# Attention output kept by feature and divided by its softmax sums in the dense stages, with two PSUM banks for the sums of y

## The reference

```python
x = x + attn_a(layernorm(x), W_attn, W_proj)    # softmax(causal q k^T / 4), times a decay by distance, times v, times W_proj
x = x + ffn(layernorm(x), w1, b1, w2, b2)       # weights binarised: sign(w) * mean|w| of the row; exact gelu
x = x + attn_b(layernorm(x), Wq, bq, ..., Wo, bo, gamma, beta)   # softmax(causal), times v, times Wo, layernorm of the result
x = x + ffn(layernorm(x), w1, b1, w2, b2)
```

## Time and profile before

| | |
|---|---|
| median of 3 runs | 2737.45 us (2736.65 to 2740.8) |
| the profiled execution | 2736.11 us, span 2734.4 us |
| granted TensorE clock, mean | 0.959 |
| PE busy | 2454.8 us, 90% |
| DVE busy | 1958.3 us, 72% |
| ACT busy | 1515.6 us, 55% |
| POOL busy | 1052.5 us, 38% |
| DMA | 171.03 MB, mean 63 GB/s |

### The profile page before, as it was taken

How to read it: one execution, slowest core, us unless ns; L and a number is a source line. 1 busy time by engine, 2 the same in 40 slices (tenths; PEclk the granted TensorE clock), 3 DMA queues, 4 the chain that set the end, 5 groups by cost and what they waited for, 6 DMA issues and landing times. The chain is left out here.

```text
span 2734.4 us, 44488 instructions
## 1 busy us (share of the span) xinstructions
PE 2454.8 (90%) x13984; PEld 1404.0 (51%) x13984; DVE 1958.3 (72%) x4863; ACT 1515.6 (55%) x3309; POOL 1052.5 (38%) x1274
## 2 busy tenths in 40 slices
PE   4959999999999999969997599999999999997788
PEld 2535545454544545437774355555555555553676
DVE  5667787777787777716663588888888888870786
ACT  1218576776767685734332056666666666664333
POOL 0037777777777777751221301000101001011653
PEclk8969999999999999989998589999999999998999
DMA  4994142332505050033544751423505234102110
GB/s 134 252 144 63 24 56 36 44 51 32 70 11 75 13 69 6 5 114 77 125 96 98 111 75 16 64 38 44 70 15 72 32 51 62 18 7 99 47 54 31
DMA packets 181847, 171.03 MB, mean 63 GB/s; under 512 B 90352, under 2 KB 131056, under 8 KB 180848
## 3 DMA queue, kind: packets, MB, share of 16 engines
q1 hardware_dynamic: 181616, 168.18, 35.0%
HBM read 105.98 MB, written 61.08 MB: 61 GB/s over the span
## 5 line engine op out<-in xcount | busy, mean ns | idle before, releaser
L704 POOL TENSOR_TENSOR att_a_wd<-att_a_wt,decay 128x256 f32<-128x256 f32 (+3 forms) x896 | 754.6, 873 | 259.8 <-PE att_a_po L907 122.7
L742 ACT ACTIVATE att_b_wt<-att_b_ps 128x512 f32<-128x512 f32 (+3 forms) x1280 | 589.4, 539 | 354.6 <-PE att_b_ps L882 352.6
L782 DVE TENSOR_REDUCE att_a_mpart<-att_a_pm 128x1 f32<-128x512 f32 x768 | 513.5, 687 | 132.2 <-PE att_a_pm L860 129.0
L782 DVE TENSOR_REDUCE att_b_mpart<-att_b_pm 128x1 f32<-128x512 f32 x768 | 503.7, 686 | 109.7 <-PE att_b_pm L860 107.7
L860 PE MATMUL att_a_pm<-att_a_kop,att_a_qop 128*128 128x512 f32 (+3 forms) x1280 | 522.6, 426 | 55.6 <-DMA att_a_qop<-att_a_qop 28.2
L742 ACT ACTIVATE att_a_wt<-att_a_ps 128x512 f32<-128x512 f32 (+3 forms) x896 | 430.8, 506 | 218.1 <-PE att_a_ps L885 131.6
L860 PE MATMUL att_b_pm<-att_b_kop,att_b_qop 128*128 128x512 f32 (+3 forms) x1280 | 503.0, 408 | 36.6 <-DMA att_b_qop<-att_b_qop 29.9
L882 PE MATMUL att_b_ps<-att_b_qop,att_b_kop 128*128 128x512 f32 (+3 forms) x1280 | 453.2, 383 | 6.6 <-ACT att_b_wt L742 3.4
L722 POOL TENSOR_SCALAR_AFFINE_SELECT att_b_wt<-att_b_wt 128x512 f32<-128x512 f32 x128 | 81.6, 637 | 867.1 <-ACT att_b_wt L742 867.1
L860 PEld LDWEIGHTS att_a_pm<-att_a_kop,att_a_qop 128*128 128x128 f32 x1280 | 240.6, 193 | 324.6 <-DVE att_a_mpart L782 130.2
L860 PEld LDWEIGHTS att_b_pm<-att_b_kop,att_b_qop 128*128 128x128 f32 x1280 | 246.3, 194 | 277.1 <-DVE att_b_mpart L782 112.0
(11 more groups left out here) (174 smaller groups left out, 2622.6 us busy)
## 6 DMA issues: line engine op xcount, KB each, us to landing
att_a_kop<-qk SPq DMA_DIRECT2D x128, 128.0 KB, 7.7
att_a_qop<-qk SPq DMA_DIRECT2D x128, 128.0 KB, 8.0
att_b_kop<-qk SPq DMA_DIRECT2D x128, 128.0 KB, 6.2
att_b_qop<-qk SPq DMA_DIRECT2D x128, 128.0 KB, 6.8
qk<-qkv_a_qk_hi SPq DMA_DIRECT2D x32, 256.0 KB, 4.7
qk<-qkv_a_qk_lo SPq DMA_DIRECT2D x32, 256.0 KB, 4.5
qk<-mid_qk_hi SPq DMA_DIRECT2D x32, 256.0 KB, 4.0
qk<-mid_qk_lo SPq DMA_DIRECT2D x32, 256.0 KB, 4.5
```

The costliest lines, as they stand in the source:

```text
L704: pool.tensor_tensor(wd[:, kq % 2, j, a:z], wt[:, kq % buffers, j, a:z], keep["decay"][:, u:u + z - a], ALU.mult).then_inc(w_decayed, 1)
L742: act.activation(wt[:, kq % buffers, j, a:CH], pe_[:, seen % EBANKS, 0:CH - a], ACT.Exp)\
L782: dve.tensor_reduce(mpart[:, c, piece, u:u + 1], pm[:, n % MBANKS, 0:w], AX.X, ALU.max, negate=True).then_inc(m_reduced, 1)
```

## The change

The attentions no longer turn and divide y. `O` copies the chunk's strips to `y[:, c % 2]`, and SP stores each head's 16 rows and its row of sums as they lie (8 DMAs for a chunk in place of one). `YT` and `YN` are gone, with their cost in the plan; PSUM's `px` is gone, and `po` has two banks, taken in turn by chunk. In att_a the far sums are turned on DVE (`FT`, one 32x32 block transpose for a chunk) and stored to DRAM by four DMAs.

The dense stages load y by feature, and the sums copied to 16 partitions for each head: one DMA for y and 16 for the sums of a chunk, 16 more for the far sums of half the chunks of mid. POOL adds the far sums (mid only), DVE takes the reciprocal of 128x1024 sums and multiplies y by it into `yt`. The eight transposes on PE and ACT's copy are gone.

```diff
@@ attention_plan
-        cost = PV_TIME if item[0] in ("PO", "PV", "YT") else 0.0
+        cost = PV_TIME if item[0] in ("PO", "PV") else 0.0
...
-            follow(number + 3, GH - 1, ("YT", c))
@@ spaced
-                follow((8, 0.0, ("FE", c)), (11, 0.0, ("FM", c)))
+                follow((8, 0.0, ("FE", c)), (11, 0.0, ("FM", c)), (14, 0.0, ("FT", c)))
@@ attention
-        pm, pe_, po, px = ps("pm", [P, MBANKS, CH]), ps("ps", [P, EBANKS, CH]), ps("po", [P, CH]), ps("px", [P, CH])
+        pm, pe_, po = ps("pm", [P, MBANKS, CH]), ps("ps", [P, EBANKS, CH]), ps("po", [P, 2, CH])
@@ attention, sync
+                    if item[0] == "O":
                         c = item[1]
-                        sp.wait_ge(y_ready, done(g, c))
...
+                        sp.wait_ge(o_kept, done(g, c) + 2)
+                        for j in range(GH):
+                            h, cols = GH * (g % NG) + j, slice(c * CH, (c + 1) * CH)
+                            sp.dma_start(dram["y"][g // NG, h, :, cols], y[STRIP * j:STRIP * j + HD, c % 2, :])\
+                              .then_inc(y_out[c % 2], 16)
+                            sp.dma_start(dram["sums"][g // NG, h:h + 1, cols],
+                                         y[STRIP * j + HD:STRIP * j + HD + 1, c % 2, :]).then_inc(y_out[c % 2], 16)
@@ attention, scalar
-                        if done(g, c) > 1:
-                            act.wait_ge(y_turned, done(g, c) - 1)
-                        act.activation(y[:, :], po[:, :], ACT.Copy).then_inc(o_kept, 1)
+                        act.wait_ge(y_out[c % 2], Y_DMAS * (2 * g + c // 2 + 1))
+                        act.activation(y[:, c % 2, :], po[:, c % 2, :], ACT.Copy).then_inc(o_kept, 1)
@@ attention, vector
-            dve.memset(po[:, :], 0.0).then_inc(o_kept, 1)
+            dve.memset(po[:, :, :], 0.0).then_inc(o_kept, 2)
...
+                    if item[0] == "FT":
+                        _, d, c = item
+                        n = FARS.index(c)
+                        dve.wait_ge(f_total, len(FARS) * (g + d) + n + 1)
+                        dve.wait_ge(f_out[n], F_DMAS * (g + d + 1))
+                        dve.transpose(frow[:, n, :], ftotal[:, n, :]).then_inc(f_turned, 1)
@@ attention, tensor
-                    if item[0] == "YT":
...
-                            mm = pe.transpose(px[:, t * P:(t + 1) * P], y[:, t * P:(t + 1) * P], keep["ident"][:, :])
@@ dense, sync: load_y
-                sp.dma_start(y[:, G % 2, :, :], at(dram["y"], 0, G)).then_inc(y_in[G % 2], 16)
+                sp.dma_start(y[:, G % 2, :, :], dram["y"][b].rearrange("(k h) d t -> (h d) k t", k=KT)[:, :, cols])\
+                  .then_inc(y_in[G % 2], 16)
+                for h in range(H):
+                    part = slice(HD * (h % (H // KT)), HD * (h % (H // KT) + 1))
+                    sp.dma_start(sums[part, G % 2, h // (H // KT), :],
+                                 dram["sums"][b, h:h + 1, cols].to_broadcast([HD, CH])).then_inc(y_in[G % 2], 16)
...
@@ dense, gpsimd
+                if item[0] == "Y" and G in FAR_CHUNKS:
...
+                    pool.tensor_tensor(sums[:, G % 2, :, :], sums[:, G % 2, :, :], far_sums[:, :, :], ALU.add)\
+                        .then_inc(sums_ready, 1)
@@ dense, tensor
-                if item[0] == "Y":
-                    pe.wait_ge(y_in[par], 16 * (G // 2 + 1))
-                    wait_turned(item)
-                    turn(y[:, par, :, :], y_turned)
@@ dense, vector
+                if item[0] == "Y":
+                    dve.wait_ge(y_in[par], Y_LOADS * (G // 2 + 1))
+                    if G in FAR_CHUNKS:
+                        dve.wait_ge(sums_ready, FAR_CHUNKS.index(G) + 1)
+                    if G:
+                        dve.wait_ge(projected, G)
+                    dve.reciprocal(sums[:, par, :, :], sums[:, par, :, :]).then_inc(inverted, 1)
+                    dve.wait_ge(inverted, G + 1)
+                    dve.tensor_tensor(yt[:, :, :], y[:, par, :, :], sums[:, par, :, :], ALU.mult).then_inc(yt_ready, 1)
```

More of the change, by code:

```diff
@@ L516, in attention_plan @@
             timed.append((t, 1, len(timed), (item[0], 0, *item[1:])))
-    plan = [item for _, _, _, item in sorted(timed)]
-    return [x for item in plan for x in ((item, ("YN", *item[1:])) if item[0] == "YT" else (item,))]
+    return [item for _, _, _, item in sorted(timed)]
 def spaced(m, decayed):
@@ L579, in attention @@
         f_done, f_diff, f_factor, f_prod, f_total = (sm(n) for n in ("f_done", "f_diff", "f_factor", "f_prod", "f_total"))
-        y_turned, y_summed, y_inverse, y_ready = sm("y_turned"), sm("y_summed"), sm("y_inverse"), sm("y_ready")
+        f_padded, f_turned = sm("f_padded"), sm("f_turned")
+        f_out = [sm(f"f_out{i}") for i in range(NC - 2)] if decayed else []
         w_masked, w_turn = sm("w_masked"), sm("w_turn")
@@ L603, in steps @@
             step(GROUPS - 1, GROUPS // 2 - 1, 1, LAST)
+        Y_DMAS = 16 * 2 * GH
+        F_DMAS = 16 * (P // SQUARE)
         def done(g, c):
@@ L635, in _ @@
             for i in range(2):
-                sp.sem_inc(y_out[i], 16)
+                sp.sem_inc(y_out[i], Y_DMAS)
+            for f in f_out:
+                sp.sem_inc(f, F_DMAS)
             for c in range(NC):
@@ L683, in _ @@
             for i in range(2):
-                sp.wait_ge(y_out[i], 16 * (GROUPS * NC // 2 + 1))
+                sp.wait_ge(y_out[i], Y_DMAS * (GROUPS * NC // 2 + 1))
+            for f in f_out:
+                sp.wait_ge(f, F_DMAS * (GROUPS + 1))
         @block.gpsimd
@@ L862, in step @@
                         mm.then_inc(m_scores, 1)
-                    if item[0] == "YT":
-                        c = item[1]
-                        pe.wait_ge(o_kept, done(g, c) + 1)
-                        if done(g, c) > 1:
-                            pe.wait_ge(y_ready, done(g, c) - 1)
-                        for t in range(TB):
-                            mm = pe.transpose(px[:, t * P:(t + 1) * P], y[:, t * P:(t + 1) * P], keep["ident"][:, :])
-                        mm.then_inc(y_turned, 1)
                     if item[0] == "S":
@@ L1002, in dense_plan, with dense @@
     return plan
-def dense(nc, name, x_src, x_dst, w, norm, weights, biases, keep, dram):
+def dense(nc, name, x_src, x_dst, w, decayed, norm, weights, biases, keep, dram):
     with ExitStack() as ctx:
@@ L1020, in dense @@
         ROTATION = [item for item in PLAN if item[0] in "HQ"]
-        TURNS = [item for item in PLAN if item[0] in "YXZ"]
+        TURNS = [item for item in PLAN if item[0] in "XZ"]
         PAIRS_USED = [item for item in PLAN if item[0] in "PVB"]
@@ L1066, in dense @@
         N_W = 16 * (1 + 3 * bool(norm))
+        Y_LOADS, F_LOADS = 16 * (1 + H), 16 * H
+        FAR_CHUNKS = [G for G in range(CHUNKS) if decayed and far(G % NC, decayed)]
         N_QKV = 16 * (len(weights) + 3) if qkv else 0
@@ L1071, in load_y @@
             def load_y(G):
+                b, c, cols = G // NC, G % NC, slice(G % NC * CH, G % NC * CH + CH)
                 if G >= 2:
-                    sp.wait_ge(y_turned, G - 1)
-                sp.dma_start(y[:, G % 2, :, :], at(dram["y"], 0, G)).then_inc(y_in[G % 2], 16)
+                    sp.wait_ge(yt_ready, G - 1)
+                sp.dma_start(y[:, G % 2, :, :], dram["y"][b].rearrange("(k h) d t -> (h d) k t", k=KT)[:, :, cols])\
[5 more added lines that the diff above has]
+                if G in FAR_CHUNKS:
+                    n = FAR_CHUNKS.index(G)
+                    if n:
+                        sp.wait_ge(sums_ready, n)
+                    for h in range(H):
+                        part = slice(HD * (h % (H // KT)), HD * (h % (H // KT) + 1))
+                        row = dram["far"][b, h // GH, c, TB * (h % GH):TB * (h % GH) + TB, :].rearrange("t p -> (t p)")
+                        sp.dma_start(far_sums[part, h // (H // KT), :], row_of(row).to_broadcast([HD, CH]))\
+                          .then_inc(far_in, 16)
             def load_x(G):
@@ L1197, in wait_turned @@
                     what, G = BEFORE[item]
-                    if what == "Y":
-                        pe.wait_ge(yt_ready, G + 1)
-                    elif what == "X":
+                    if what == "X":
                         pe.wait_ge(hi_ready, G + 1)
@@ L1299, in _ @@
                 par = G % 2
-                if item[0] == "Y":
-                    act.wait_ge(y_turned, G + 1)
-                    if G:
-                        act.wait_ge(projected, G)
-                    act.activation(yt[:, :, :], pt[:, :, :], ACT.Copy).then_inc(yt_ready, 1)
                 if item[0] == "X":
@@ L1459, in build @@
             "v": dram("v", (B, NG, NC, P, TB * GH * (HD + 1)), F32),
-            "y": chunks(dram("y", (B, T, D), F32)),
+            "y": dram("y", (B, H, HD, T), F32),
+            "sums": dram("sums", (B, H, T), F32),
+            "far": dram("far", (B, NG, NC, UNITS, P), F32),
```

(4 more changed lines are left out.)

54 lines of the change are left out of this document (24 added, 30 removed).

## The result

| | before | changed |
|---|---|---|
| median | 2737.99 us of 4 runs (2736.65 to 2740.8) | 2829.72 us of 4 runs (2826.4 to 2831.65) |
| profiled execution | 2736.11 us, span 2734.4 us | 2831.65 us, span 2829.9 us |
| granted TensorE clock, mean | 0.959 | 0.930 |

The changed kernel takes 1.0332 times as long, with a 95% interval of 1.0314 to 1.035: 92 us more. The forecast was slower, 2810 us, with a range of 2765 to 2848.

A forecast was written before the change was run, and what follows sets the result against it. PE was taken to bound attention and mid, PE and DVE waiting for each other in end. Attentions -56, their ends +3, mid +33 and +34, end +21 and +39 sum to +74: 2810 us, range 2765 to 2848.

The forecast's parts named there:

- The price of one `Y`: Dense stages, on DVE: reciprocal 6.55 us plus product 1.22 us, 7.8 us for a chunk, 16 times.
- Rivals 1 and 3: Dense stages: reciprocal streams one element a cycle, total 2727 us (8%); or costs two cycles more per element, 2841 us (10%).
- The attentions: Both attentions: dropped transposes and the second bank gain 56 us; late stores at their ends cost 3 us.
- Rival 4: Attentions gain little, -16 in place of -56, as waits move to ACT and DVE: 2850 us; chance 7%.
- Start of mid: Before mid's first FFN matmul: more DMA issues, two DVE divisions and a later projection cost 33 us.
- Loop of mid: Mid's six loops with a division: PE's projection starts 5.7 us later in each, +34 us.
- Start of end: Start of the end stage: later loads and DVE's first three divisions cost 21 us.
- Loop of end: End's loop, five times: DVE has no gap, so the whole 7.8 us goes to each loop, +39 us.
- Rival 2: Dense loops: PE and DVE run apart and give half back, costing 3 and 4 us each; 2775 us; chance 17%.

The follow-up runs named there:

- Experiment 1: The changed kernel without DVE's reciprocal of the sums, only the product (output differs): 2725.12 us, ratio 0.994 to the kernel before.
- experiment 2: The changed kernel with one PSUM bank instead of two for the sums of y in the attentions: 2858.39 us, ratio 1.0425 to the kernel before.
- experiment 4: The changed kernel with a chunk's sums loaded by 2 transfers and far sums by 4, instead of 16 each: 2830.48 us, ratio 1.0326 to the kernel before.
- experiment 7: The changed kernel with unused transposes filling PE's loop stalls, 60 in mid and 72 in end: 2812.47 us, ratio 1.027 to the kernel before.

## Why the prediction was right, and where it was short

- **The price of one `Y`: right.** 6.55 us for the reciprocal and 1.22 for the product, as worked out from two small sizes. Rivals 1 and 3 are out. The Trainium skill ("VectorE: DVE Perf Modes", First, the fixed hardware budget) gives the reciprocal a repeat count of 8; the estimate made from it at 8 cycles an element is 8.5 us, and the trace has 6.55. Experiment 1 shows that this price, with what the clock adds, is 107 us.
- **The attentions: right.** -25.9 and -23.7, -50 in sum, where -56 + 3 = -53 was forecast; the start of mid came between 1166.0 and 1171.7 us in kernels that differ ahead of it at most in where the far sums are stored (all but experiment 2), so the 3 us are within what one profile tells. Rival 4 is out. The bank's share is shown by experiment 2 (25 us, forecast 24). The other 25, where the forecast had 32 less 3 for the transposes and the late stores, are what is left over: they were not run by themselves, and DVE's and ACT's relief is in them too.
- **Start of mid: right.** DVE began 26.3 us after the first load (17.3 before), +9.0 for 9.3; the first matmul of the FFN came 63.3 us after it (30.4 before), +32.9 for 32.6. Of the 9.3 the size was right, but the working took it from SP's time to issue: experiment 4 had 4 issues in place of the 32 and lost as much, so the traffic of the copied rows holds the weights up by itself. That both come to 9 us is luck as far as the forecast goes.
- **Loop of mid: short.** Mid's +76.0 less 32.9 leaves 43 where the step "loop of mid: +34" had 34. PE waited 7.07 us and the projection began when the working had it, right behind `R`; that it then takes 5.3 to 5.9 us in place of 3.62 was not in the term. That the clock holds was assumed without being said. With the clock up (experiment 7) the same remainder of mid is 32.8 us.
- **Start of end: right.** The first matmul of the FFN came 8.8 us later, PE then waited 12.7 us for `g_lo` behind `Y(2)` (2.6 before), and the third projection, at which the loop begins, came 70.5 us after the first load in place of 49.9: 20.6 for 21.
- **Loop of end: short** by the same cause. 69.1 less 20.6 is 48.5 for 39, or 9.7 us a loop in place of 7.8. Experiment 7 gives the split: with the clock up a chunk takes 31.9 us, as forecast (38.7 us in all), and 1.6 to 2.1 us more without.
- **Rival 2**, PE and DVE apart, giving half back: out. In mid PE waited 7 us in each loop and had its work behind the stall as before; nothing was made good later.

So the mechanism stood and two terms of the sum, the loop of mid and the loop of end, were undersized, by 9 and 9.5 us. These 18 us are TensorE's clock, a term that the sum left out: experiment 7 took 17 off with PE kept busy and nothing else changed. The ends of the terms, added again, give +33 to +111 and not +34 to +112, which changes no reading.

## What to carry to other kernels

Look at how many different values an expensive elementwise operation works on: dividing after a broadcast costs one inverse per copy, and one packed reciprocal ahead of the broadcast (3.35 us a stage in place of 52.4) turned a loss of 92 us into a gain of 14. When an engine gets a new item in a loop, place it where that engine already waits, with a buffer more if need be; in end the same 1.2 us product cost 3 us a chunk in one place and nothing in another. And a stall of PE can cost more than its length, since the matmuls behind it may run at the lower clock: 1.6 to 2.1 us more for each stall of 7 to 8 us here, nothing for waits of 0.5 to 1.1 us. Look at the granted clock behind every wait that a change puts ahead of a dense stretch of matmuls.
